# Turning the normalized rows back: eight TensorE transposes a batch replaced by sixteen 32x256 VectorE block transposes

## What is computed

```python
soma = gelu(x @ Wsoma.T + bsoma)
gate = sigmoid(temporal @ Wtemp.T + btemp)    # temporal: eight causal moving averages, blended
out  = (soma * gate) @ Wout.T                 # per token, 256 features
x2   = x + (out - mean(out)) / sqrt(var(out) + 1e-5) * gamma + beta
```

```python
y = x2 + g0 * (wa * ffn_a(x2) + wb * ffn_b(x2)) + g1 * s0(x2) + g2 * s1(x2) + g3 * s2(x2)
```

## Time and profile before

| | us |
|---|---|
| median of 3 runs | 1045.18 (1044.25 to 1045.28) |
| the profiled execution: span from first to last instruction | 1044.1 |
| PE busy | 1036.7 (99%), 4850 matmuls |
| DVE busy | 756.8 (72%) |
| ACT busy | 405.0 (39%) |
| DMA | 214 GB/s mean |

### The profile page before, as it was taken

The page is one execution under the profiler, slowest core; times in us unless marked ns, Lnnn a source line. Parts: engine busy times, 40 slices in busy tenths (PEclk is TensorE's granted clock), DMA queues, the critical chain, the costliest instruction groups (busy, mean ns, idle before and its releaser), DMA issues.

```text
span 1044.1 us, 12751 instructions
## 1 busy us (share of the span) xinstructions
PE 1036.7 (99%) x4850; PEld 861.1 (82%) x4850; DVE 756.8 (72%) x1260; ACT 405.0 (39%) x663; POOL 16.3 (2%) x26
## 2 busy tenths in 40 slices
PE   8999999999999999999999999999999999999998
PEld 5688888888888888888888888888888888888898
DVE  6989977799547986389764996559955599545236
ACT  8654555423443234422344223433334432423232
POOL 1200000000000000000000000000000000000000
PEclk9999999999999999999999999999999999999999
DMA  5388999786354754466544664546645465355582
GB/s 213 121 313 275 312 356 356 282 324 240 131 192 167 257 181 162 162 238 210 197 164 163 231 235 152 185 162 242 208 154 201 163 235 204 146 201 191 203 323 90
DMA packets 38302, 223.02 MB, mean 214 GB/s; under 512 B 4514, under 2 KB 5282, under 8 KB 16610
## 3 DMA queue, kind: packets, MB, share of 16 engines
q1 hardware_dynamic: 35938, 209.63, 56.1%
q0 software_dynamic: 2304, 12.58, 3.2%
HBM read 188.51 MB, written 33.69 MB: 213 GB/s over the span
## 4 chain that ended last, share of the span: by engine, by line
PE 96%; DMA 2%; DVE 2%; issue 0%; SPq 0%; ACT 0%; DVEq 0%
PE ps_up L665 14%; PE ps_up L695 14%; PE ps_up L696 14%; PE ps_down L737 14%; PE ps_down L741 14%; PE ps_down L738 14%; PE ps_aux L658 2%; PE ps_aux L659 2%; PE ps_aux L660 2%; DMA wi<-split_wi 1%; DVE y L1633 1%; PE ps_aux L837 1%; PE ps_aux L834 1%; PE ps_aux L833 1%; PE ps_aux L822 1%; PE ps_aux L818 1%
## 5 line engine op out<-in xcount | busy, mean ns | idle before, releaser
L1065 ACT ACTIVATE hid_hi<-ps_up 128x512 fp32r<-128x512 f32 (+1 forms) x336 | 193.5, 576 | 507.8 <-PE ps_up L665 507.6
L1306 DVE SCALAR_TENSOR_TENSOR hid_lo<-ps_up,hid_hi 128x512 fp32r<-128x512 f32 (+1 forms) x336 | 220.1, 658 | 228.9 <-ACT hid_hi L1065 227.5
L695 PE MATMUL ps_up<-x_hi_all,wi 128*128 128x512 f32 (+1 forms) x660 | 250.8, 382 | 0.4 <-DMA wi<-split_wi 0.4
L696 PE MATMUL ps_up<-x_hi_all,wi 128*128 128x512 f32 (+1 forms) x660 | 249.9, 380 | 0.0
L737 PE MATMUL ps_down<-hid_hi,wo 128*128 128x512 f32 (+1 forms) x640 | 245.3, 384 | 0.1
L738 PE MATMUL ps_down<-hid_hi,wo 128*128 128x512 f32 (+1 forms) x640 | 245.1, 384 | 0.0
L665 PE MATMUL ps_up<-x_lo_all,wi 128*128 128x512 f32 (+1 forms) x660 | 197.4, 380 | 0.2 <-DVE x_lo_all L1297 0.2
L741 PE MATMUL ps_down<-hid_lo,wo 128*128 128x512 f32 (+1 forms) x640 | 193.9, 384 | 0.0
L695 PEld LDWEIGHTS ps_up<-x_hi_all,wi 128*128 128x128 f32 x660 | 124.1, 188 | 24.1 <-DMA wi<-split_wi 0.8
L696 PEld LDWEIGHTS ps_up<-x_hi_all,wi 128*128 128x128 f32 x660 | 124.1, 188 | 23.0
L665 PEld LDWEIGHTS ps_up<-x_lo_all,wi 128*128 128x128 f32 x660 | 122.0, 188 | 24.3 <-DVE x_lo_all L1297 0.4
(11 more groups left out here) (248 smaller groups left out, 855.1 us busy)
## 6 DMA issues: line engine op xcount, KB each, us to landing
wi<-split_wi SPq DMA_DIRECT2D x70, 1024.0 KB, 4.8
wo<-split_wo SPq DMA_DIRECT2D x70, 1024.0 KB, 4.9
modb<-mod_scratch SPq DMA_DIRECT2D x28, 512.0 KB, 4.6
split_wi<-wi SPq DMA_DIRECT2D x10, 1024.0 KB, 7.3
split_wo<-wo SPq DMA_DIRECT2D x10, 1024.0 KB, 7.6
xt<-in_x SPq DMA_DIRECT2D x8, 512.0 KB, 5.8
split_wi<-ex POOLq DMA_DIRECT2D x4, 1024.0 KB, 8.6
split_wo<-ex POOLq DMA_DIRECT2D x4, 1024.0 KB, 6.0
```

What stands on the lines that cost most here:

```text
L695: pe.matmul(ps, w_hi, x2_hi[:, parity, c, tokens], start=c == 0, stop=False)
L696: pe.matmul(ps, w_lo, x2_hi[:, parity, c, tokens], start=False, stop=False)
L1065: act.activation(hid_hi[:, k % NU, tokens], ps_up[k % NU][:, tokens], ACT.Relu).then_inc(hid_hi_ready, 1)
L1306: dve.scalar_tensor_tensor(hid_lo[:, k % NU, tokens], ps_up[k % NU][:, tokens], 0.0, f32(hid_hi[:, k % NU, tokens]), ALU.max, ALU.subtract ...
```

## The change

Four things change, for n = 1 to 7 only:

1. PE's step `turn` is gone from the plans and the code.
2. DVE gets four steps `turn0` to `turn3`. Step `turn a` takes the 32 partitions of quarter a of `normed` (32 tokens of every group of 128) and writes four blocks, one to each partition quarter b of `gates`, which is free by then. Each is one instruction over 32 partitions and 256 elements, that turns eight 32x32 squares. In `PLANS` they stand at 30.5, 31, 31.5 and 32; in `FIRST_PLANS` at 32, 32.5, 33 and 33.5.
3. ACT's `turn` waits for all sixteen blocks and reads `gates` (SBUF) in place of `ps_aux` (PSUM), at the same place in its list.
4. `ln_norm` no longer ends with the wait and the `nop`; the wait stands at the start of `turn0`.

```diff
 PLAN_TENSOR = {
...
-    25.5: ["tgate"], 28.5: ["out"], 32: ["turn"],
+    25.5: ["tgate"], 28.5: ["out"],
...
-    24.5: ["temp_lo"], 26.5: ["sg"], 27: ["sg_lo"], 29: ["ln_stats"], 30: ["ln_norm"], 33.5: ["x2"], 35: ["x2_lo"],
+    24.5: ["temp_lo"], 26.5: ["sg"], 27: ["sg_lo"], 29: ["ln_stats"], 30: ["ln_norm"], 30.5: ["turn0"], 31: ["turn1"], 31.5: ["turn2"], 32: ["turn3"], 33.5: ["x2"], 35: ["x2_lo"],
...
+        untouched = normed[:, :, :].rearrange("p t (c b j) -> p b c t j", c=CT, b=4)
+        turned = gates[:, :, :].rearrange("p c (t a j) -> p a c t j", t=TT, a=4)
...
-                elif step == "turn":
-
-                    pe.wait_ge(normed_ready, n)
-                    for c in range(CT):
-                        if later(p.aux[c]["turn"]):
-                            pe.wait_ge(aux_free[c], p.aux[c]["turn"])
-                        for t in range(TT):
-                            mm = pe.transpose(ps_aux[c][:, t * P:(t + 1) * P], normed[:, t, c * P:(c + 1) * P], ident[:, :])
-                        mm.then_inc(aux_ready[c], 1)
...
-                        act.wait_ge(aux_ready[c], p.aux[c]["turn"] + 1)
-                        act.activation(x2[:, p.n_parity, c, :], ps_aux[c][:, :], ACT.Identity, bias=col(C_BETA, c),
-                                       scale=col(C_GAMMA, c)).then_inc(aux_free[c], 1)
+                        act.wait_ge(turned_ready, n * 16)
+                        act.activation(x2[:, p.n_parity, c, :], gates[:, c, :], ACT.Identity, bias=col(C_BETA, c),
+                                       scale=col(C_GAMMA, c)).then_inc(scaled_ready, 1)
...
-                    dve.wait_ge(aux_free[1], p.aux[1]["out"] + 1)
-                    dve.nop().then_inc(normed_ready, 1)
+                elif step.startswith("turn"):
+                    a = int(step[-1])
+                    if a == 0:
+                        dve.wait_ge(sg_split, n)
+                        for m in range(CT):
+                            dve.wait_ge(aux_free[m], p.aux[m]["out"] + 1)
+                    for b in range(4):
+                        dve.transpose(turned[quarter(b), a], untouched[quarter(a), b]).then_inc(turned_ready, 1)
                 elif step == "x2":
                     for c in range(CT):
-                        dve.wait_ge(aux_free[c], p.aux[c]["turn"] + 1)
+                        dve.wait_ge(scaled_ready, (n - 1) * CT + c + 1)
```

More of the change, by code:

```diff
@@ L79 @@
     "sync": from_slot(PLAN_SYNC, 8, {1: ["mod"], 1.5: ["modb0", "modb1"]}),
-    "tensor": {0.5: ["mod"], 1.5: ["wgate"], 27.5: ["tgate"], 30: ["out"], 33.5: ["turn"]},
+    "tensor": {0.5: ["mod"], 1.5: ["wgate"], 27.5: ["tgate"], 30: ["out"]},
     "scalar": {0.5: ["mod"], 2: ["wgate"], 26: ["temp_hi"], 28: ["tgate"], 29: ["sg_hi"],
@@ L83 @@
     "vector": {2: ["wgate_scan", "gated"],
-               26: ["temp_lo"], 28.5: ["sg"], 29: ["sg_lo"], 30.5: ["ln_stats"], 31.5: ["ln_norm"], 35: ["x2"], 36: ["x2_lo"],
+               26: ["temp_lo"], 28.5: ["sg"], 29: ["sg_lo"], 30.5: ["ln_stats"], 31.5: ["ln_norm"], 32: ["turn0"], 32.5: ["turn1"], 33: ["turn2"], 33.5: ["turn3"], 35: ["x2"], 36: ["x2_lo"],
                37.5: ["next_x_lo"]},
@@ L313, in build @@
         rstd_ready = sem("rstd_ready")
-        normed_ready = sem("normed_ready")
         turned_ready = sem("turned_ready")
+        scaled_ready = sem("scaled_ready")
         x2_ready = sem("x2_ready")
@@ L409, in build, with quarter @@
         open_total_of = open_traces[3]
+        untouched = normed[:, :, :].rearrange("p t (c b j) -> p b c t j", c=CT, b=4)
+        turned = gates[:, :, :].rearrange("p c (t a j) -> p a c t j", t=TT, a=4)
         def x_of(n):
             return xt[n % 2][:, :, :]
+        def quarter(i):
+            return slice(i * P // 4, (i + 1) * P // 4)
         def raw_part(i):
```

## The result

The changed kernel takes 1065.92 us (median of 4 runs, 1062.20 to 1068.49), against 1045.03 for the kernel before at the same time: ratio 1.0195, 95% interval 1.0172 to 1.0219. The forecast was 1053.7, range 1045 to 1062. So the sign was right, and the loss, 20.9 us, is more than twice the 8.5 forecast. The profiled execution has a span of 1065.7, 21.6 over that of before.

The account below looks back on a forecast made before the run. PE, busy for 99% of the span, was taken as the bound. Stalls less PE's gain, 6 x (16t - 4.9) + (16t - 4.1) - 6.2, gave +8.5 us at t = 0.43: 1045.18 + 8.5 = 1053.7 us, range 1045 to 1062.

Parts of the forecast that it names:

- t: Time on DVE from one block transpose's start to the next; taken as 0.43 us, bounds 0.34, 0.50 and 0.70.
- 112t - 39.7: Whole change in time, all seven batches' stalls less PE's gain: +8.5 us at t = 0.43, zero at 0.354.
- PE's gain (6.2 us): Seven turns gone from PE at 0.89 us each, all gained if no wait takes their place: 6.2 us.
- The hold (no overlap between quarters): On DVE, a transpose writing to another partition quarter starts only when the one before is over: t = 0.43 us.
- Rival (a): DVE's transposes overlap as ordinary neighbours do, t under 0.354: sum -2.3 us, about 1042.9; chance 0.12.
- (c): DVE's transposes run at half the rate, t = 0.70: +38.7 us, 1083.9; chance 0.08.
- (b): DVE's transposes take two elements a cycle or less fixed cost, t = 0.30: 1039.7 us; chance 0.06.
- 16t - 4.9: PE's stall per batch, 1 to 6, waiting for relu_lo behind DVE's sixteen transposes: 2.0 us at t = 0.43.
- The DMA queues: Costed at nothing: their waits count PE's and DVE's steps of the mixture and are not moved past anything.
- 16t - 4.1: Batch 0's stall of PE: 16t - 4.6 for relu_lo(36), some 0.5 us more at `down(37)` and `up(0)`.
- ACT at nothing: ACT's `turn` and the relu behind it add no PE wait at `down(35)`: 0.5 us left whatever t is.
- Rival (d): The turn's time on PE was no cost: at most 6.2 us off the gain, 1059.9 at t = 0.43; chance 0.02.

Follow-up runs that it names:

- run 1: The changed kernel without its block transposes (turn0 a nop, the other three steps empty, the turning back left out): 1038.54 us, ratio 0.9938.
- run 2: The kernel before with the sixteen transposes added on DVE at the change's places, result unread, PE still turning: 1060.17 us, ratio 1.0142.
- Run 11: The changed kernel with each transpose cut into two of 128 elements with the same input and output quarter, 32 in a batch: 1079.88 us.
- run 4: The changed kernel with four transposes over all 128 partitions in place of sixteen over 32, the crossing of quarters left out: 1040.26 us, ratio 0.9968.
- run 3: The changed kernel with each of the sixteen transposes over half its elements, the other half left out: 1046.95 us, ratio 1.0013.
- run 6: The changed kernel with the six multiply-adds into gpart in slot 26 instead of 31 for batches 1 to 6: 1044.48 us, ratio 1.0001.
- run 5: The changed kernel with ACT's and DVE's splitting of expert tiles 4 to 7 three slots later: 1063.57 us, ratio 1.0182.
- run 10: The changed kernel with the turn between batches 0 and 1 back on PE, multiply-adds still at slot 31: 1059.37 us, ratio 1.0131.
- run 8: The changed kernel with the moves of run 5 and run 6 together: 1044.17 us, ratio 1.0003.

## Why the prediction was right and wrong

The 21.6 us between the two profiled spans, by its own terms: six batches at 1.6, 9.6; four falls of the clock at 1.6, 6.4; and 5.6 for batch 0 (as what is left; its waits of 0.50, 1.86, 0.91 and 2.87, less the turn's 0.89, are 5.3). Forecast were 8.5: 1.1 for each of the six and 1.9 for batch 0.

**The steps that failed** are two things priced at nothing, the clock behind the forecast waits and the DMAs that wait for DVE in batch 0. One size, t, was too small besides, and that alone would have done no harm: at t = 0.467 the sum 112t - 39.7 gives +12.6 us, 1057.8. With 6.4 for the clock and 2.9 for the DMAs it gives 1067.1, and the profiled execution took 1067.32.

**PE's gain (6.2 us): right**, run 1. But it is no sum of its own. Where PE waits for DVE, a shorter PE lengthens the wait by nearly as much (run 2). The formula has this, since 0.89 is in every stall; the sentence that all of it is gained "if no wait takes its place" is the whole matter.

**The hold (no overlap between quarters): right**, and it decides, as the prediction said. Run 11 shows it directly, and run 4 what is saved without it. Rival (a) falls, and (c) with it (0.70); (b) falls by the length of 436 ns.

**t = 0.43: mis-sized.** It is 0.467: the element rate was right, the fixed part is 0.17 and not 0.16, and a held start comes 0.03 behind the end, not 0.01. That is 0.037 by 16 by 7: some 4 us by the sum's 112t, 3.1 of them in batches 1 to 6 (0.5 each, measured). With 0.467 the formula 16t - 4.9 gives 2.57, and the profile has 1.6 + 0.89 = 2.5. So it held; run 3 tells the same from the other side. In batch 1 the wait forecast at `down(35)` came in two, 0.46 and 1.45, and the batch costs the same 1.6. The estimate from the Trainium skill's page (VectorE: DVE Perf Modes, "The three transpose paths"), 0.45, was nearer than mine.

**The clock: missing from the prediction, 6.4 us.** It read the full level in all slices of before and had no term for a fall, though it forecast idles of 2 us on an engine that had had almost none. The waits forecast, "some 15 us in all", are the 15.3 of the profile; what came behind them was not forecast.

**Batch 0's DMA chain: missing, 2.9 us in this profile.** "The DMA queues ... not moved past anything" held for SP's: PE waits for none of its weights in the change. But the moves of the experts' tiles on POOL wait for splits on DVE; the prediction counted those splits as time on DVE ahead of relu_lo(36), and never asked who waits for them. The late split cost PE 2.87 where the transfers were slow too, and nothing in the profiles of runs 2 and 6. It is a part of the median of 1065.92 only as often as that happens, which no run counts. The rest of batch 0 came as forecast: 16t - 4.1 is 3.4 at 0.467, and PE's waits for `hid_lo` and `y` are 2.4 and 0.9.

**ACT at nothing: right.** PE never waits for `hid_hi` in the changed kernel, ACT waits for the blocks instead, and its two activations are little longer from SBUF (808 ns beside 779). Rival (d) falls with run 1: no idle was there to be filled.

Together 0.037 on t (3.1 in batches 1 to 6), batch 0 (3.7, of which 0.6 is t and the rest mainly the DMA chain) and the clock (6.4) make the 13.1 us that were missing.

What stays open: why a wait of 2.20 brings a fall in some batches and not in others. It isn't the same batches in each profile. Open too is why the same transfers take over 3 us more in one profile than in another.

## What to carry to other kernels

An op moved off the bounding engine gains its time only where the receiving engine has room *ahead of the next thing that the first one wants*; count the receiver's list from its last forced start to that point, and look for other work there that can stand earlier (six multiply-adds moved by five slots turned +20.9 us into nothing, and with batch 0 left alone into -5.4). Follow every instruction that is made late to all who wait for it, DMAs on other queues too. And where TensorE is the bound, price a forecast wait of 2 us at the wait and, as an estimate from these runs, a part of another 1.6.

## What the runs showed of the hardware that was not expected

- Falls of the granted clock (to 1.2 GHz, 3.4 us each, 1.6 us of time) behind waits of PE in batches 2 to 6: none behind five waits of 1.51 to 1.56 (run 2); behind 3 of 5 of 2.20, in each of three profiles (the change, runs 5 and 10); behind 5 of 5 of 3.16 (run 11). In batch 0 it fell behind waits of 1.85 to 1.9 in runs 2, 5, 6 and 8, and stayed up behind 1.86 in the change and behind 2.10 in run 11; it fell at the waits for `modh` of 2.54 (run 3), 2.87 (the change) and 3.16 (run 11), and not at 1.13 (run 4). In batch 1 it fell behind 1.94 in run 11 and not behind 1.45 in the change.
- Sixteen block transposes over 32 partitions that cross quarters take 7.5 us of VectorE (16 x 0.467), eight 128x128 transposes on TensorE 0.89 for the same data; four over all partitions, which don't cross, 1.5 (two take 0.76).
- A block transpose that writes to another quarter than the one before starts 0.03 us after that one's end. One that stays in the quarter starts before it: 0.07 us before for 128 elements (run 11), 0.08 for 256 over all partitions (run 4).
- An fp32 transpose of 32 partitions by 256 takes 436 ns and one of 128 partitions 421: the number of partitions costs nothing, an element of each 1.05 ns (134 ns for 128).
